# Layer 0's attention scored, turned and valued over the keys that a fixed sparse mask lets through

## What is computed

```
h = layernorm(x) * (1 + scale) + shift            # scale, shift from the condition
q = rope(h @ Wq.T)           # 16 heads of 32
latent = h @ Wkd.T           # 128 wide
k = rope(latent @ Wku.T); v = latent @ Wvu.T      # 4 heads of 32, each shared by 4 query heads
hidden(q, k) = (|k - q| > 64 and k % 64 != 0) or k // 128 > q // 128
y = softmax(where(hidden, -inf, q k / sqrt(32))) @ v
x = x + y @ Wo.T
```

## Time and profile before

| | |
|---|---|
| time, median of 3 runs (lowest, highest) | 2551.07 us (2549.32, 2553.27) |
| the profiled execution's own time | 2549.21 us |
| its span, first to last instruction | 2547.1 us |
| granted TensorE clock, mean | 0.977 |
| TensorE busy | 2401.9 us (94%), 13000 matmul records |
| VectorE, ScalarE, POOL busy | 1200.0, 1077.9, 265.9 us |
| chain that ended last | TensorE 87%, ScalarE 6%, VectorE 5% |

### The profile page before, as it was taken

The page is one execution under the profiler, slowest core; times in us unless marked ns, Lnnn a source line. Parts: engine busy times, 40 slices in busy tenths (PEclk is TensorE's granted clock), DMA queues, the critical chain, the costliest instruction groups (busy, mean ns, idle before and its releaser), DMA issues.

```text
span 2547.1 us, 32014 instructions
## 1 busy us (share of the span) xinstructions
PE 2401.9 (94%) x13000; PEld 1497.4 (59%) x13000; DVE 1200.0 (47%) x2466; ACT 1077.9 (42%) x2407; POOL 265.9 (10%) x222
## 2 busy tenths in 40 slices
PE   6889999999999899999999989999999899999998
PEld 2445545455454587888877544545455567888733
DVE  2465564544446353444443254637366555444323
ACT  2465565544335331111113155638467662222374
POOL 2332021121110100000001010101001110000021
PEclk9899999999999999999999979999999899999999
DMA  9100000000001000000001000000001010000001
GB/s 332 45 17 17 1 24 18 10 1 9 9 1 51 1 25 25 25 25 25 25 7 67 17 1 1 1 1 1 1 1 34 17 50 34 17 17 1 1 17 50
DMA packets 45235, 64.95 MB, mean 25 GB/s; under 512 B 8368, under 2 KB 21952, under 8 KB 45088
## 3 DMA queue, kind: packets, MB, share of 16 engines
q1 hardware_dynamic: 44112, 60.38, 7.3%
q0 software_dynamic: 976, 2.51, 0.3%
HBM read 52.66 MB, written 4.19 MB: 22 GB/s over the span
## 4 chain that ended last, share of the span: by engine, by line
PE 87%; ACT 6%; DVE 5%; POOL 1%; issue 1%; DMA 0%; SPq 0%; DVEq 0%; POOLq 0%; ACTq 0%
PE banks L1024 34%; PE banks L388 22%; PE banks L663 9%; PE banks L655 8%; PE banks L679 5%; PE banks L689 2%; ACT sb_Pr L765 2%; PE banks L486 2%; PE banks L261 1%; PE banks L426 1%; ACT sb_PT L770 1%; PE banks L561 1%; PE banks L569 1%; DVE sb_hN L352 1%; DVE sb_Pr L735 1%
## 5 line engine op out<-in xcount | busy, mean ns | idle before, releaser
L1024 PE MATMUL banks<-sb_HH,sb_Ws 128*128 128x512 f32 x1536 | 491.7, 394 | 12.7 <-DVE sb_HL L941 7.3
L663 PEld LDWEIGHTS banks<-sb_ident,sb_Pr 128*128 128x128 f32 x2176 | 244.6, 144 | 201.0 <-issue 87.7
L765 ACT ACTIVATE sb_Pr<-sb_Pr,sb_nmax 128x512 f32<-128x512 f32 (+3 forms) x512 | 322.3, 633 | 48.0 <-DVE sb_nmax L735 47.1
L663 PE MATMUL banks<-sb_ident,sb_Pr 128*128 128x128 f32 x2176 | 318.6, 286 | 22.0 <-ACT sb_PT L770 11.3
L1024 PEld LDWEIGHTS banks<-sb_HH,sb_Ws 128*128 128x128 f32 x1536 | 290.0, 189 | 77.5 <-issue 17.6
L1024 PE MATMUL banks<-sb_hidH,sb_Ws 128*128 128x512 f32 x1024 | 332.0, 394 | 0.0
L735 DVE CUSTOM_DVE_ANT_0 sb_Pr<-banks,sb_bias 128x512 f32<-128x512 f32 (+3 forms) x512 | 279.2, 582 | 103.2 <-PE banks L655 102.5
L770 ACT ACTIVATE sb_PT<-banks 128x512 f32<-128x512 f32 (+3 forms) x320 | 169.2, 529 | 346.5 <-PE banks L663 345.5
L1024 PE MATMUL banks<-sb_HL,sb_Ws 128*128 128x512 f32 x768 | 300.1, 391 | 0.0
L742 DVE COPY sb_PT<-banks 128x512 f32<-128x512 f32 (+3 forms) x320 | 194.5, 608 | 199.6 <-PE banks L663 199.2
L655 PE MATMUL banks<-sb_R 32*128 32x512 f32 (+4 forms) x1280 | 256.3, 593 | 29.6 <-DVE sb_nmax L735 13.4
(11 more groups left out here) (128 smaller groups left out, 2505.9 us busy)
## 6 DMA issues: line engine op xcount, KB each, us to landing
sb_staged<-in_L_cond_Wfc SPq DMA_DIRECT2D x16, 512.0 KB, 4.2
sb_wada<-in_L_cond_Wada SPq DMA_DIRECT2D x6, 1024.0 KB, 6.0
sb_x<-in_x SPq DMA_DIRECT2D x4, 1024.0 KB, 9.9
sb_staged<-in_L_cond_Wg SPq DMA_DIRECT2D x8, 512.0 KB, 3.5
sb_staged<-in_L_cond_Wu SPq DMA_DIRECT2D x8, 512.0 KB, 4.5
sb_staged<-in_L_cond_Wd SPq DMA_DIRECT2D x8, 512.0 KB, 3.6
out_x<-sb_x SPq DMA_DIRECT2D x4, 1024.0 KB, 4.5
sb_R<-sb_R SPq DMA_DIRECT2D x60, 64.0 KB, 2.0
```

What stands on the lines that cost most here:

```text
L663: mm = e.transpose(bank[:, j * P:(j + 1) * P], k.Pr[:, n % 6, j * P:(j + 1) * P], k.ident[:])
L765: ins = e.activation(prob, prob if s.biased else k.bank(n % 4)[:, 0:s.width(u)], ACT.Exp, bias=s.stat(k, k.nmax, b, u), scale=-1.0 if s.bi ...
L1024: mm = e.matmul(bank, lhsT, rhs, start=i == 0, stop=i == len(mats) - 1)
```

## The change

Layer 0's `Heads` becomes `NearHeads`. Its scores are 128 wide for tile 0 and 193, 195, 197 for tiles 1 to 3: own tile, 64 keys in front, and 1, 3 or 5 of the older keys, each part with a matmul of its own. It turns two tiles instead of i + 1: the own tile, and the other 65 to 69 keys together. Values take the two. The values of those other keys, in this order on partitions 0 to 68, come from a new eighth group of `proj0` (number 7: six matmuls from the latent, one VectorE copy to `VN`), and the values of a batch and the next norm wait for it. The mask is packed in the same order: [128, 4, 200], which a DMA of 0.4 MB loads in the place of the old one. Layer 2 keeps its mask.

```diff
--- before.py
+++ after.py
@@ -385,7 +385,8 @@
             for key in needs:
                 for due in after(*key):
                     e.wait_ge(*due)
-            mm = e.matmul(bank[:, columns], lhsT, rhs, start=start, stop=stop)
+            out = bank[:, columns] if isinstance(columns, slice) else bank[columns]
+            mm = e.matmul(out, lhsT, rhs, start=start, stop=stop)
         mm.then_inc(k.done["pe"], 1)
 
     def put_waits(s, e, b, g, after):
@@ -611,13 +612,13 @@
 
 
 
-    def __init__(s, name, H, PT, q, kk, v, out, vhead, bias_loaded, tiles_of, q_ready, k_ready, v_ready, out_free,
+    def __init__(s, name, H, PT, q, kk, v, out, vhead, bias, tiles_of, q_ready, k_ready, v_ready, out_free,
                  prob_fresh=(), turned_fresh=(), k_loaded=None):
         s.name, s.H, s.PT, s.q, s.k, s.v, s.out, s.vhead = name, H, PT, q, kk, v, out, vhead
-        s.bias_loaded, s.tiles_of = bias_loaded, tiles_of
+        (s.bias, s.bias_loaded), s.tiles_of = bias or (None, None), tiles_of
         s.q_ready, s.k_ready, s.v_ready, s.out_free = q_ready, k_ready, v_ready, out_free
         s.prob_fresh, s.turned_fresh = prob_fresh, turned_fresh
-        s.k_loaded, s.biased = k_loaded, bias_loaded is not None
+        s.k_loaded, s.biased = k_loaded, bias is not None
         s.dv = D // H
         s.per = H // C
         s.units = [(c, ip, i, hl) for c in range(C) for ip in range(2) for i in (2 * ip, 2 * ip + 1)
@@ -733,7 +734,7 @@
                 if u == 0 and b == 0:
                     e.wait_ge(s.bias_loaded, 16)
                 ins = e.tensor_tensor_reduce(k.Pr[:, n % 6, 0:s.width(u)], S,
-                                             k.bias[:, s.units[u][2], 0:s.width(u)],
+                                             s.bias[:, s.units[u][2], 0:s.width(u)],
                                              -1.0, 3.0e38, ALU.add, ALU.min, s.stat(k, k.nmax, b, u))
             else:
                 ins = e.tensor_reduce(s.stat(k, k.nmax, b, u), S, AX_X, ALU.max, negate=True)
@@ -776,6 +777,76 @@
                     e.wait_ge(*due)
             ins = e.activation(s.out(b, u), s.tab.at[(s.name, b, "values", 2 * u)], ACT.Copy)
         ins.then_inc(k.done["act"], 1)
+
+
+class NearHeads(Heads):
+
+
+
+
+    def __init__(s, *args, near, **more):
+        s.near = near
+        super().__init__(*args, **more)
+
+    def width(s, u):
+        i = s.units[u][2]
+        return 3 * P // 2 + 2 * i - 1 if i else P
+
+    def pe(s, k, e, b, kind, u, after):
+        if kind == "scores":
+            c, _, i, hl = s.units[u]
+            bank = s.tab.claim(e, s, b, kind, u, after)
+            for due in after(*s.q_ready(b, c)):
+                e.wait_ge(*due)
+            for due in after(*s.k_ready(b, c)):
+                e.wait_ge(*due)
+            if u == 0:
+                e.wait_ge(*s.k_loaded(b))
+            rows = slice(hl * s.dv, (hl + 1) * s.dv)
+            q, kk = s.q(b, c)[rows, i * P:(i + 1) * P], s.k(b, c)
+            mm = e.matmul(bank[:, 0:P], q, kk[rows, i * P:(i + 1) * P], start=True, stop=True)
+            if i:
+                e.matmul(bank[:, P:P + 64], q, kk[rows, i * P - 64:i * P], start=True, stop=True)
+                mm = e.matmul(bank[:, P + 64:s.width(u)], q, kk[rows, 0:128 * i - 127:64], start=True, stop=True)
+        elif kind == "turn":
+            for due in after(s.name, b, "exp", u):
+                e.wait_ge(*due)
+            bank = s.tab.claim(e, s, b, kind, u, after)
+            prob = k.Pr[:, (s.first[b] + u) % 6, :]
+            mm = e.transpose(bank[:, 0:P], prob[:, 0:P], k.ident[:])
+            if s.units[u][2]:
+                mm = e.transpose(bank[0:s.width(u) - P, P:2 * P], prob[:, P:s.width(u)], k.ident[:])
+        elif kind == "values":
+            c, ip = divmod(u, 2)
+            n = s.tab.group_number[(s.name, b, u)]
+            for due in after(s.name, b, "copy", (u + 1) * s.G - 2):
+                e.wait_ge(*due)
+            for due in after(s.name, b, "copy", (u + 1) * s.G - 1):
+                e.wait_ge(*due)
+            for due in after(*s.v_ready(b)):
+                e.wait_ge(*due)
+            bank = s.tab.claim(e, s, b, kind, u, after)
+            for half in range(2):
+                i = 2 * ip + half
+                queries, others = slice(half * P, (half + 1) * P), 64 + 2 * i - 1
+                for hl in range(s.per):
+                    mm = e.matmul(bank[hl * s.dv:(hl + 1) * s.dv, i * P:(i + 1) * P], s.v(b, i, s.vhead(c, hl)),
+                                  s.PT[:, n % 2, hl, 0, queries], start=True, stop=i == 0)
+                for hl in range(s.per) if i else ():
+                    mm = e.matmul(bank[hl * s.dv:(hl + 1) * s.dv, i * P:(i + 1) * P],
+                                  s.near(b, i, s.vhead(c, hl))[0:others, :], s.PT[0:others, n % 2, hl, 1, queries],
+                                  start=False, stop=True)
+        else:
+            super().pe(k, e, b, kind, u, after)
+            return
+        mm.then_inc(k.done["pe"], 1)
+
+    def turned(s, k, b, u):
+        _, ip, i, hl = s.units[u]
+        n = s.tab.group_number[(s.name, b, s.group(u))]
+        half, kinds = i - 2 * ip, 2 if i else 1
+        return (s.PT[:, n % 2, hl, 0:kinds, half * P:(half + 1) * P],
+                s.tab.at[(s.name, b, "turn", u)][:, 0:kinds * P].rearrange("p (j q) -> p j q", q=P))
 
 
 def seated(k, tab, segments):
@@ -1184,6 +1255,8 @@
         wout3 = place("Wout", 27648, [P, C, D])
         hide = place("experts", 13312, [P, 2 * C, T])
         Y = place("Y", 0, [P, 3, C, T])
+        mask0 = place("mask0", 8192, [P, TT, 200])
+        VN = place("VN", 8992, [P, 2, 3, P])
 
         high = lambda b, c: HH[b][:, c, :]
         low = lambda b, c: HL[b][:, c, :]
@@ -1335,9 +1408,19 @@
         load0 = (l_w[0], 64)
         norm0 = SideNorm("norm0", k.xs, hN, modc(0), modc(4), eps5[:, 0:1], lambda b, c: [],
                          lambda b: [("proj0", b - 1, "mm", 5)] if b else [],
-                         lambda b: [("proj0", b - 1, "mm", 6)] if b else [],
+                         lambda b: [("proj0", b - 1, "mm", 7)] if b else [],
                          mod_ready=[("ada", 0, "mod", 0), ("ada", 0, "mod", 1)], x_loaded=lambda b: (l_x[b], 16))
         v0 = lambda b: V01[:, b % 2, :]
+
+        def near_values(b):
+
+            mats = []
+            for i in range(1, TT):
+                o, ready = slice((i - 1) * P, i * P), [("proj0", b, "put", 0)]
+                mats.append(((slice(0, 64), o), latent[:, i * P - 64:i * P], wvu, True, True, ready))
+                mats.append(((slice(64, 63 + 2 * i), o), latent[:, 0:128 * i - 127:64], wvu, True, True, ready))
+            return mats
+
         proj0 = SideLinear("proj0", [
             Group(lambda b: product(wkd, 0, hsrc, shifted("norm0", b)), "act", act_copy(lambda b: latent),
                   free=lambda b: [("norm0", b, "var", 0)], load=load0)] + [
@@ -1347,19 +1430,21 @@
                               [("proj0", b, "put", 0)]) for j in range(TT)], "dve", dve_copy(v0),
                   free=v_free("heads0"))] + [
             Group(lambda b: [(full, wku, latent, True, True, [("proj0", b, "put", 0)])], "act",
-                  act_copy(lambda b: rk(b, C - 1)), free=qk_free("heads0"))])
+                  act_copy(lambda b: rk(b, C - 1)), free=qk_free("heads0")),
+            Group(near_values, "dve", lambda e, b, bank: e.tensor_copy(
+                VN[0:69, b % 2, :, :], bank[0:69, 0:3 * P].rearrange("p (i m) -> p i m", i=3)), free=v_free("heads0"))])
         rope0 = SideRope("rope0", lambda b: [rk(b, C - 1)] + [rq(b, c) for c in range(C)],
                          lambda b, g: ("proj0", b, "put", g or 6), perm[:, 0, :],
                          lambda b: [("rope0", b - 1, "add", 4)] if b else [], loaded=lambda b: (l_rope, 16 * 3))
-        heads0 = Heads("heads0", 16, PT, rq, rk, lambda b, j, h: v0(b)[:, j * P + 32 * h:j * P + 32 * h + 32], attended,
-                       lambda c, hl: c, l_bias[0], lambda i: i + 1, lambda b, c: ("rope0", b, "add", 1 + c),
-                       lambda b, c: ("rope0", b, "add", 0), lambda b: ("proj0", b, "put", 5), out_free("heads0"),
-                       k_loaded=lambda b: (l_k, 16 * 15 * (b + 1)), turned_fresh=[("ada", 0, "turn", BLOCKS - 1)])
+        heads0 = NearHeads("heads0", 16, PT, rq, rk, lambda b, j, h: v0(b)[:, j * P + 32 * h:j * P + 32 * h + 32], attended,
+                       lambda c, hl: c, (mask0, l_bias[0]), lambda i: 2 if i else 1, lambda b, c: ("rope0", b, "add", 1 + c),
+                       lambda b, c: ("rope0", b, "add", 0), lambda b: ("proj0", b, "put", 7), out_free("heads0"),
+                       near=lambda b, i, h: VN[:, b % 2, i - 1, 32 * h:32 * h + 32], k_loaded=lambda b: (l_k, 16 * 15 * (b + 1)), turned_fresh=[("ada", 0, "turn", BLOCKS - 1)])
         post0 = post(0, wo0, load=(l_wo0, 16))
 
```

(14 more changed lines are left out.)

## The result

The kernel after takes 2570.04 us (median of four runs, 2566.74 to 2573.31), against 2552.17 for the kernel before: ratio 1.0069, 95% interval 1.0047 to 1.0091. It is 18 us slower, where 12 faster was forecast, and it lies 0.04 us above the range's upper end of 2570. The profiled executions lie further apart than the medians, 2571.4 against 2547.1 of span, 24.3 us: before's took 2549.21, just under the lowest of its timed runs (2549.32), after's was the slowest of its own (2573.31).

A forecast was written before the change was run, and what follows sets the result against it. TensorE was taken to bound layer 0's attention (busy 368 of 396.1 us). Turning -21, its waits -6, values -10, scores +16 and near group +9 gave -12 us from 2551.1: 2539 us, range 2505 to 2570 for 8 in 10.

The forecast's parts named there:

- waits at the turns: TensorE's waits around layer 0's transposes, for copies and the divide, shrink as other engines' operations narrow: -6 us.
- score rounds, undisturbed: Layer 0's score rounds without waits: 48 us now, 90 us then, as 48 rounds of 1.74 and 16 of 0.43.
- waits inside the rounds: Waits for score banks inside layer 0's rounds: 30 us now, mostly gone with late-starting heads, 4 left.
- the price list: TensorE costs from the timeline: 0.11 us a transpose, 1.7 ns a values column, 0.107 + w/600 + 0.11 us a score round.
- the six waiting instructions: On a score strip, six waiting instructions may be passed; the next head starts when only six of the one before are left.
- the delay of 0.32: In a three-part score round, each next head starts 0.32 us after the one before.
- the round of 1.74: A three-part score round of four heads: 3x0.32 + 0.67 + 0.11 = 1.74 us.
- Rival 1: Score rounds: all four heads still overlap, rounds cost 0.78 us; sum -44, 2507 us; chance 0.27.
- rival 2: Score rounds: heads go one after another, rounds cost 2.70 us; sum +31, 2582 us; chance 0.13.
- my case: Score rounds of 1.74 us with six waiting as the limit: scores +16 us, kernel 2539 us; chance 0.47.
- Rival 3: Gain outside scores is hidden behind copies and exponentials; half of the 37 us stays, about 2555 us; chance 0.13.
- the turn waits were my mistake: Sign: if the second head's delay is 0.32 us and the time still above 2552, the turn-wait term was wrong.

The follow-up runs named there:

- the run with the split undone: Kernel after with one score matmul a head over all 128(i+1) keys, as in the kernel before; 2523.69 us, ratio 0.9892 to the kernel before.
- Parts in turn: Kernel after with its three score matmuls issued part by part over the four heads instead of head by head; 2524.14 us, ratio 0.9893 to the kernel before.

## Why the prediction was wrong

Three steps of the sum failed. The waits were to shrink by 32 us (26 inside the rounds, 6 at the turns), and they shrank by 15. The granted clock of the side work stood at nothing and cost 9. The start of the lead, beyond the near group's own matmuls, stood at nothing and cost 5. By its own steps, in the profiled executions (from start to start; sum 24, measured 24.3):

| term | forecast | profiled |
|---|---|---|
| fewer transposes | -21 | -21 (192 x 0.107) |
| waits at the turns | -6 | +2 |
| values | -10 | -8.5 |
| score rounds, undisturbed | +42 | +43 (48 x 1.75 + 16 x 0.43 against 48) |
| waits inside the rounds | -26 (30 to 4) | -17 (32 to 15.5) |
| near group's matmuls | +9 | +8 |
| start of the lead, beyond those | 0 | +5 |
| 512-wide side matmuls (clock) | 0 | +9 |
| spread, rest | 0 | +3.5 |

**Right, and shown:** the price list, the six waiting instructions, the delay of 0.32, the round of 1.74, the transposes and the near group's own price. Rival 1 (0.78) and rival 2 (2.70) fall by the round; the time landed between my case and rival 2 by other terms. Rival 3 falls by the run with the split undone.

**Waits inside the rounds.** "The waits inside mostly go, since a head that starts late finds its bank free, and I leave 4" failed. In the 47 wide rounds that can be counted singly (the first follows the first narrow one directly) it held: excess over the shortest 18.6 us before, 5.3 after. But 12 us had stood in the narrow rounds of 128 columns, which do not stagger, and 8.0 are still there, and the first rounds wait 2 us as before.

**Waits at the turns.** I took -6 because the copies and exponentials shrink, and they do: maximum and exponential at their widest are now

```profile
L736 DVE CUSTOM_DVE_ANT_0 sb_Pr<-banks,sb_mask 128x197 f32<-128x197 f32 x64 | 21.1, 360 | 14.3 <-PE banks L810 14.1
```

```profile
L766 ACT ACTIVATE sb_Pr<-sb_Pr,sb_nmax 128x197 f32<-128x197 f32 x62 | 27.7, 451 | 4.3 <-DVE sb_nmax L736 4.3
```

360 and 451 ns against 685 and 712. Yet what turning takes above 0.107 us a transpose is 39.1 us before and 40.6 after, and between 35.4 and 43.3 in the twelve kernels of the experiments; with only the split undone, where the score rounds are as before and the other engines' work is narrow, it is again 39. So it hardly depends on how long those operations are. The earlier trace rows held the reason. Of TensorE's idle time ahead of turning, 11.8 us before and 9.9 after, the divide has the most, 5.1 and 5.2, and it is as wide as it was; only the waits for copies fell, from 6.2 to 4.6. No wait for an exponential is among them. Of the 39.1 and 40.6 us, 22 and 23 stand between a turn and an operation that starts over 0.4 us later: a turn behind the divide or a copy, a spread behind a copy, side work behind its own input. The other 17 or so are spread thinly over single turns. And ScalarE, now done sooner, waits for turns longer than the 70.8 us of the earlier trace rows:

```profile
ACT sb_PT L771 <- PE banks L818: 102.3, 63, 7.0
...
ACT sb_PT L771 <- PE banks L816: 31.6, 20, 4.4
```

**The clock.** The prediction has no term for it: it priced every side matmul at the full level. The granted clock of the attention fell to 0.91 and cost 9 us there. Parts in turn, the same instructions, had 0.97, so the order of issue brought it down here; by what way is open. In the lead the low clock has a part in the 5 us beside the moved block: without near group and moved block the first scores still came at 92.4, with a clock of 0.50.

**The added step.** "In batch 0 the group stands before the rope of the keys ... these 2.3 us move the start" was right. But I wrote "the steps stand closer in time" of the attention alone, and never asked what a step more does to the lead, where the same even spacing places the conditioning blocks. The prediction's own sign, "the turn waits were my mistake" if the delay is 0.32 and the time above 2552, names only 8 of the 36 us between forecast and profile.

A chance of 0.19 stood on slower. Three terms with one sign each (waits, clock, start) were taken at their best value, and their bounds were not carried into the range. Two of its numbers are also off by its own account: half way from 2539 to rival 2 is 2560, not 2570, and half of the 37 us lost (rival 3) is about 2558, not 2555.

## What to carry to other kernels

When one matmul becomes several on row strips, count the instructions a strip, four for each fp32 matmul (load, pass, load, pass): above six waiting, the strips behind it did not start here, and issuing the pieces in turn over the strips gave 46 us (36 without the near group). Three pieces of 193 to 197 columns together, issued in turn, saved nothing against one matmul of 256 to 512 columns (2524.14 and 2523.69), since every piece loads its weights again. Before adding a step to a schedule spaced evenly, look at what stands in each gap now, and leave room in the range for the granted clock, which differed here between kernels with the same instructions.

## What had not been expected of the hardware

- A strip let six waiting instructions be passed and not seven; with eight, twelve and sixteen a head the next strip starts after 0.013, 0.33 and 0.50 us.
- The granted clock can follow how the same columns are cut and ordered: 0.97 (rounds of 0.77), 0.91 (1.75) and 0.83 (2.51), and 512-wide matmuls beside them took 148, 158 and 172 us for 318. Without the near group it was 0.94 with rounds of 0.77 and of 1.75 alike.
- One and the same lead started the scores at 87.0 and 88.3 (granted clock of 40 to 50 us 1.00 and 0.92) or at 91.2 and 91.5 (0.56 and 0.54); a single profile can't price a change of the lead finer than 4 us.
- A pass of 1 to 5 columns in front of a long one costs 0.1 us a round more than behind it.
